# A graph network on one Trainium2 core: the two count banks of a step evicted at its end and stored by one transfer of four blocks

## The reference

```python
def L0(x, edge, src, dst, W_e, b_e, eps, W1, b1, gamma, beta, W2, b2):
    m = relu(edge @ W_e + b_e + x[src])                # one row of 128 for each edge
    h = segment_sum(m, dst, n) + (1.0 + eps) * x
    z = h @ W1 + b1
    z = relu((z - mean(z, 0)) * rsqrt(var(z, 0) + 1e-5) * gamma + beta)
    return z @ W2 + b2

def L1(x, src, dst, W0, b0, W1, b1, W2, b2):           # self loops are added to the edges
    deg = segment_sum(ones, dst, n); norm = rsqrt(deg)[src] * rsqrt(deg)[dst]
    for W, b in ((W0, b0), (W1, b1), (W2, b2)):
        x = relu(segment_sum((x @ W)[src] * norm, dst, n) + b)
    return x

x = layernorm(x + L0(x, edge_attr, src, dst, ...))
x = layernorm(x + L1(x, src, dst, ...))
```

## Time and profile before

| | |
|---|---|
| median of 3 runs | 3333.89 us (3331.76 to 3340.97) |
| the profiled execution | 3360.1 us, its span 3358.2 us |
| PE busy | 2531.0 us, 75% |
| DVE busy | 2436.1 us, 73% |
| PE weight loads busy | 2016.8 us, 60% |
| ACT busy | 1571.9 us, 47% |
| POOL busy | 1556.9 us, 46% |
| stores of `adj` | 392, 245.0 KB each |
| loads of edge features | 196, 256.0 KB each |

### The profile page before, as it was taken

The page is one execution under the profiler, slowest core; times in us unless marked ns, Lnnn a source line. Parts: engine busy times, 40 slices in busy tenths (PEclk is TensorE's granted clock), DMA queues, the critical chain, the costliest instruction groups (busy, mean ns, idle before and its releaser), DMA issues.

```text
span 3358.2 us, 43285 instructions
## 1 busy us (share of the span) xinstructions
PE 2531.0 (75%) x13163; PEld 2016.8 (60%) x13291; DVE 2436.1 (73%) x4239; ACT 1571.9 (47%) x2892; POOL 1556.9 (46%) x1694
## 2 busy tenths in 40 slices
PE   3666676666666666676666666666789999999998
PEld 2555555555555555555555555555578888888887
DVE  7777777777777777777777777777778885445554
ACT  3444444444444444444444444444555555445444
POOL 7666666666666666666666666665110000000111
PEclk7877877878778788777877878778889999999999
DMA  5333333333333333333333333333223332333442
GB/s 200 106 109 110 109 112 109 109 109 108 108 109 111 109 112 110 109 111 110 109 109 109 108 109 111 110 112 102 85 102 140 150 132 113 150 132 126 170 171 81
DMA packets 157600, 394.53 MB, mean 117 GB/s; under 512 B 37056, under 2 KB 100571, under 8 KB 151995
## 3 DMA queue, kind: packets, MB, share of 16 engines
q1 hardware_dynamic: 104332, 274.85, 21.8%
q0 software_dynamic: 51168, 105.71, 13.7%
q10 hardware_dynamic: 1872, 11.13, 0.8%
HBM read 286.75 MB, written 104.80 MB: 117 GB/s over the span
## 4 chain that ended last, share of the span: by engine, by line
DVE 50%; PE 27%; another core or an unknown queue 15%; issue 6%; ACT 1%; DVEq 1%; DMA 0%; POOL 0%; ACTq 0%; POOLq 0%; SPq 0%
DVE z L1272 21%; PE psE L1128 13%; PE psA L1128 12%; DVE work L1254 7%; DVE held L1266 6%; DVE work L1279 6%; DVE onehot L1260 4%; DVE work L1280 4%; PE psA L1083 1%; ACT wide L917 0%; PE psA L1052 0%; DVE acc L1284 0%; PE psE L1040 0%; PE psA L1040 0%
## 5 line engine op out<-in xcount | busy, mean ns | idle before, releaser
L775 POOL DMA_INDIRECT work<-in_x_flat,idx x1568 | 1494.5, 953 | 839.6 <-issue 421.7
L439 PE MATMUL psE<-we,work 128*128 128x256 f32 x1568 | 682.6, 584 | 216.8 <-DMA work<-in_edge_cols 147.7
L843 ACT ACTIVATE z<-psA 128x490 int32 x392 | 223.7, 571 | 1243.7 <-PE psA L1005 931.1
L1272 DVE TENSOR_SCALAR z<-iota_r,key,scale 128x490 bf16<-128x490 f16 x1568 | 716.0, 520 | 0.0
L439 PEld LDWEIGHTS psE<-we,work 128*128 128x128 f32 x1568 | 481.7, 307 | 146.6 <-issue 53.4
L1005 PE MATMUL psA<-z 128*128 128x245 bf16 x3136 | 459.1, 292 | 68.5 <-issue 64.7
L849 ACT ACTIVATE z<-iota_c,low 128x128 bf16<-128x128 f16 x1568 | 476.9, 389 | 0.0
L1284 DVE TENSOR_TENSOR acc<-psS,acc 128x144 f32 x196 | 60.3, 308 | 545.1 <-remote 543.7
L1128 PE MATMUL psE<-wide,halves 128*128 128x500 f32 (+1 forms) x2058 | 448.6, 375 | 5.8 <-ACT halves L932 5.4
L989 PE MATMUL psS<-onehot,work 128*128 128x72 f32 x3136 | 391.5, 279 | 80.9 <-DVE acc L1284 66.9
L436 PE MATMUL psE<-edge_bias,ones_b 128*128 128x512 bf16 x264 | 153.4, 581 | 395.2 <-DMA work<-in_edge_cols 304.8
(11 more groups left out here) (174 smaller groups left out, 2233.8 us busy)
## 6 DMA issues: line engine op xcount, KB each, us to landing
counts<-adjacency SPq DMA_DIRECT2D x36, 3062.5 KB, 9.9
adjacency<-work SPq DMA_DIRECT2D x392, 245.0 KB
work<-in_edge_cols SPq DMA_DIRECT2D x196, 256.0 KB
work<-in_x_flat,idx POOLq DMA_INDIRECT x1568
counts<-adjacency SPq DMA_DIRECT2D x3, 1592.5 KB, 6.6
acc<-in_x_cols ACTq DMA_DIRECT2D x1, 3136.0 KB
xn<-in_x_rows ACTq DMA_DIRECT2D x1, 3136.0 KB
x_spill<-xn SPq DMA_DIRECT2D x12, 256.0 KB, 2.2
```

The costliest lines, as they stand in the source:

```text
L439: mm = pe.matmul(psE0[0:n, 2 * q:2 * q + 2, :].rearrange("p j f -> p (j f)"), eaT[:, slot, q, 0:n], we[:, :], start=False, stop=True, skip ...
L775: gp.indirect_dma_start(gath[0:size(g), g % R, j, :], None, x_flat[:, :], bass.IndirectOffsetOnAxis(ap=idx[0:size(g), g, j:j + 1], axis=0) ...
L843: act.activation(taken[:, w % TAKEN, :, :], ring[:, bass.ds(at, 2 * HC)].rearrange("p (a n) -> p a n", a=ODD), ACT.Copy).then_inc(evac_ok, 1)
L1272: ve.tensor_scalar(hot[:, k % RB, :], iota_r[:, :, 0:2 * HC // ODD], key[:, k:k + 1], scale[:, k:k + 1], ALU.is_equal, ALU.mult).then_inc( ...
```

## The change

The unit of eviction and storing becomes the step. PE counts `chunk_mm` once a step, with the last matmul of the fourth pair, and waits for the evictions of the whole step before, ahead of its third pair (there the first bank is cleared that the step before may still hold). ACT makes the low one-hots first and evicts both banks behind each other at the step's end. DVE takes both apart as before, one in the middle of a step and one after the window's add; `full` has four slots. SP stores two banks, four blocks, with one transfer of 3920 bytes a partition, one register and one wait for the store before; the ring of semaphores has two. The tables hold for each step the two banks behind the block that the next step starts in, and one place for the store, so `adj` has 323 blocks a row instead of 321, and the first real block is number 4. DVE clears two banks at the start instead of one. `full` moves down in `work`, into space that the edge features' slots leave free.

```diff
--- before.py
+++ after.py
@@ -29,10 +29,9 @@
 LB = 4
 RE = 2
 RING = 5
-BEHIND = 2
 ENDS = "DAPDADAPDADAP"
 TAKEN = 4
-SLOTS = 3
+SLOTS = 4
 ODD = 5
 FLAG_STEP = 20
 PC = 7
@@ -82,14 +81,14 @@
     NB = cdiv(N, 512)
     NB4 = cdiv(NT, 4)
     NB8 = cdiv(NT, 8)
-    assert G == GF + 1 and REST % P == P // 2 and NBLK * D <= NP and 2 * HP == J and NT % PC == 0 and 2 * HC <= FREE_COL and F == P
+    assert G == GF + 1 and NBLK % 2 == 1 and REST % P == P // 2 and NBLK * D <= NP and 2 * HP == J and NT % PC == 0 and 2 * HC <= FREE_COL and F == P
     assert len(ENDS) == NB4 and FE == P // 2 and H == 2 * P and 0 < G1 < P and CH - NCHK == XB and GF * J < NCHK <= CH and J == 8 and RB % J == 0
 
     hws = nc.dram_tensor("hws_scratch", (NP, F), F32)
     x1s = nc.dram_tensor("x1_spill", (NP, F), F32)
     degs = nc.dram_tensor("degree_scratch", (NT, P), F32)
     tscr = nc.dram_tensor("table_scratch", (2 * P, 4 * HP), I32)
-    adj = nc.dram_tensor("adjacency", (P, NBLK + 8, HB), U8)
+    adj = nc.dram_tensor("adjacency", (P, NBLK + 10, HB), U8)
 
     with ExitStack() as ctx:
         def sb(name, shape, dt=F32):
@@ -186,7 +185,7 @@
 
         hot = zf[:, 0:RB * HC].bitcast(BF16).rearrange("p (r n) -> p r n", r=RB)
         lows = zf[:, RB * HC:RB * HC + LB * J * P // 2].bitcast(BF16).rearrange("p (s q n) -> p s q n", s=LB, q=J)
-        full_at = 4096 + RE * J * P
+        full_at = 4096 + RE * HP * P
         full = work[:, full_at:full_at + SLOTS * 2 * HC].bitcast(U16).rearrange("p (s b h n) -> p s b h n", s=SLOTS, b=2, h=2)
         taken_at = RB * HC + LB * J * P // 2
         taken_row = 2 * HC // ODD
@@ -263,7 +262,7 @@
         chunk_mm = sem("chunk_mm")
         evac_ok = sem("evac_ok")
         apart_ok = sem("apart_ok")
-        stored = [sem(f"stored{i}") for i in range(SLOTS)]
+        stored = [sem(f"stored{i}") for i in range(2)]
         mlp_mm = sem("mlp_mm")
         z_ok = sem("z_ok")
         bn_ok = sem("bn_ok")
@@ -696,22 +695,22 @@
                              tscr[0:G, 3 * HP + i * HQ:3 * HP + (1 + i) * HQ].rearrange("g (r i) -> r g i", r=1)).then_inc(tab_in, 16)
             sp.wait_ge(tab_in, 48)
 
-            def store(w, at):
-                sp.wait_ge(apart_ok, w + 1)
-                if w >= 1:
-                    sp.wait_ge(stored[(w - 1) % SLOTS], 16 * ((w - 1) // SLOTS + 1))
-                sp.dma_start(adj[:, bass.ds(at, 2), :].rearrange("p a n -> p (a n)"),
-                             full[:, w % SLOTS, :, :, :].rearrange("p b h n -> p (b h n)").bitcast(U8)).then_inc(stored[w % SLOTS], 16)
+            def store_four(s):
+                at = number(SPE, tab[2:3, HQ * s:HQ * s + 1], 0, NBLK + 6)
+                if s == G - 1:
+                    sp.sem_inc(tab_read, 1)
+                sp.wait_ge(apart_ok, HQ * s + HQ)
+                if s >= 1:
+                    sp.wait_ge(stored[(s - 1) % 2], 16 * ((s - 1) // 2 + 1))
+                h = HQ * (s % 2)
+                sp.dma_start(adj[:, bass.ds(at, 4), :].rearrange("p a n -> p (a n)"),
+                             full[:, h:h + HQ, :, :, :].rearrange("p s b h n -> p (s b h n)").bitcast(U8)).then_inc(stored[s % 2], 16)
 
             for s in range(G + 1):
                 if s + RE < G:
                     load_ea(sp, s + RE)
                 if s >= 1:
-                    at = numbers(SPE, tab[2:3, HQ * (s - 1):HQ * s], 0, NBLK + 6)
-                    if s == G:
-                        sp.sem_inc(tab_read, 1)
-                    for i in range(HQ):
-                        store(HQ * (s - 1) + i, at[i])
+                    store_four(s - 1)
 
             either(sp, SPE, 0, general_sum_sp)
 
@@ -719,8 +718,8 @@
             sp.wait_ge(deg_out, 16)
             sp.dma_start(degt[:, :], degs[:, :]).then_inc(deg_in, 16)
 
-            for i in range(SLOTS):
-                sp.wait_ge(stored[i], 16 * ((HQ * G + SLOTS - 1 - i) // SLOTS))
+            for i in range(2):
+                sp.wait_ge(stored[i], 16 * ((G + 1 - i) // 2))
             for lay in range(3):
                 for b in range(NCB):
                     q = unit(lay, b, 0)
@@ -737,7 +736,7 @@
                         sp.wait_ge(wide_ve, shares_ve(q - PIECES - 1))
                         sp.wait_ge(wide_act, q - PIECES)
                     nb = blocks_in(b)
-                    sp.dma_start(counts[b_slot(q)][:, 0:nb, :], adj[:, CB * b + 2:CB * b + 2 + nb, :]).then_inc(a_in[b_slot(q)], 16)
+                    sp.dma_start(counts[b_slot(q)][:, 0:nb, :], adj[:, CB * b + 4:CB * b + 4 + nb, :]).then_inc(a_in[b_slot(q)], 16)
                     if lay == 2 and b >= 3:
                         store_rows(sp, b - 3)
             for b in range(NCB - 3, NCB):
@@ -837,14 +836,14 @@
             rectify(0)
 
             def evacuate(w, at):
-                act.wait_ge(chunk_mm, w + 1)
+                act.wait_ge(chunk_mm, w // HQ + 1)
                 if w >= TAKEN:
                     act.wait_ge(apart_ok, w - TAKEN + 1)
                 act.activation(taken[:, w % TAKEN, :, :], ring[:, bass.ds(at, 2 * HC)].rearrange("p (a n) -> p a n", a=ODD), ACT.Copy).then_inc(evac_ok, 1)
 
             def low_hots(s):
                 if s >= LB:
-                    act.wait_ge(chunk_mm, HQ * (s - LB + 1))
+                    act.wait_ge(chunk_mm, s - LB + 1)
                 for q in range(J):
                     ins = act.activation(lows[:, s % LB, q, :], iota_c[:, 0:P], ACT.Abs, bias=low2[:, J * s + q:J * s + q + 1], scale=-1.0)
                 ins.then_inc(off_ok, 1)
@@ -859,10 +858,10 @@
                 at = numbers(ACTE, tab[1:2, HQ * s:HQ * s + HQ], 0, (RING - 1) * 512)
                 if s + 1 < G:
                     rectify(s + 1)
-                evacuate(HQ * s, at[0])
                 if s + 2 < G:
                     low_hots(s + 2)
-                evacuate(HQ * s + 1, at[1])
+                for i in range(HQ):
+                    evacuate(HQ * s + i, at[i])
 
             either(act, ACTE, 0, general_sum_act)
 
@@ -994,9 +993,8 @@
                 if p % HP == 0:
                     pe.wait_ge(low_ok, p // HP + 1)
                 pe.wait_ge(chunk_ok, 2 * p + 2)
-                w = p // 2
-                if p % 2 == 0 and w > BEHIND:
-                    pe.wait_ge(evac_ok, w - BEHIND)
+                if p % HP == 2 and p > HP:
+                    pe.wait_ge(evac_ok, HQ * (p // HP))
                 if p % 2 == 0:
                     pe.matmul(ring[:, FREE_COL:][:, bass.ds(clear_at, 1)], lows[:, (p // HP) % LB, 2 * p % J, :], ones_b[:, 0:1],
                               start=True, stop=True)
@@ -1004,7 +1002,7 @@
                     for half, at in enumerate((even_at, odd_at)):
                         mm = pe.matmul(ring[:, HC * half:][:, bass.ds(at, HC)], lows[:, (k // J) % LB, k % J, :], hot[:, k % RB, HC * half:HC * half + HC],
                                        start=(k < 1 and half < 1), stop=True, skip_group_check=(k >= 1 or half >= 1))
-                if p % 2 == 1:
+                if p % HP == HP - 1:
                     mm.then_inc(chunk_mm, 1)
 
             pe.wait_ge(base_ok, 2)
@@ -1150,7 +1148,7 @@
             link(ve.tensor_scalar(ident[:, :], iota_c[:, 0:P], pid[:, 0:1], None, ALU.is_equal))
             ve.tensor_scalar(diagonal[:, :], iota_c[:, 0:DIAG], pid[:, 0:1], float(DIAG_AT), ALU.subtract, ALU.is_equal
                              ).then_inc(ident_ok, 1)
-            link(ve.memset(psA[:, RING - 1, :], 0.0))
+            link(ve.memset(psA[:, RING - 2:RING, :], 0.0))
             ve.wait_ge(be_in, 16)
             link(ve.tensor_copy(be_parts[:, 0, :], be[:, 0, :]))
             link(ve.tensor_tensor(be[:, 1, :], be[:, 0, :], be_parts[:, 0, :], ALU.subtract))
@@ -1186,19 +1184,20 @@
             link(ve.tensor_scalar(second[:, :, :], second[:, :, :], MAGIC, None, ALU.add))
             link(ve.tensor_scalar(second[:, :, :], second[:, :, :], -MAGIC, None, ALU.add))
             upper = second[:, :, 1:HP + 1]
-            next_four = second[:, :, :].rearrange("p t (q two) -> p t q two", two=2)[:, :, 1:HQ + 1, 1]
+            after = second[:, :, HP + 1:HP + 2]
             link(ve.scalar_tensor_tensor(odd[:, :, :], upper, -2.0, here_, ALU.mult, ALU.add))
             link(ve.tensor_tensor(bank[:, :, 0:HP], upper, odd[:, :, :], ALU.add))
             link(ve.tensor_copy(bank[:, :, HP:2 * HP], upper))
             link(ve.scalar_tensor_tensor(bank[:, :, 2 * HP:3 * HP], upper, 1.0, odd[:, :, :], ALU.add, ALU.add))
-            link(ve.tensor_scalar(bank[:, :, 3 * HP:3 * HP + HQ], next_four, RING - 1.0, None, ALU.add))
+            for i in range(HQ):
+                link(ve.tensor_scalar(bank[:, :, 3 * HP + i:3 * HP + i + 1], after, float(RING - HQ + i), None, ALU.add))
             link(ve.tensor_scalar(round_of[:, :, :], bank[:, :, :], 1.0 / RING, 0.5 / RING - 0.5, ALU.mult, ALU.add))
             link(ve.tensor_scalar(round_of[:, :, :], round_of[:, :, :], MAGIC, None, ALU.add))
```

(6 more changed lines are left out.)

## The result

The kernel after takes 3343.2 us (median of 17 runs, 3340.0 to 3346.8), the kernel before 3336.2 us (17 runs, 3331.8 to 3341.0): a ratio of 1.002, 95% interval 1.0014 to 1.0027. That is 7.1 us more, where 1.4 us were forecast. It is inside the forecast's own range of 3328 to 3344, near its upper end, and inside the 0.3% that counts as no change, but the interval of the ratio excludes 1. So the question is where some 6 us beyond the forecast come from.

A forecast was written before the change was run, and what follows sets the result against it. The prediction took PE's late release, held back by eight gathers a step, as the bound. Terms of 0 for the steps, +0.17 at the start and +1.23 at the end gave 3335.3 us on the median 3333.9; range 3300 to 3350, no-change 3328 to 3344.

The forecast's parts named there:

- What bounds the kernel: Stage of 196 steps: PE's updates reaching three engines late set the 11.85 us step, not DVE's 9.0 us of work.
- The loop of release: In each step: release, a batch of eight gathers, about 2 us until PE's updates get through, release.
- the `find_bad` step: Step with 13 more small DVE instructions: DVE's wait shrank from 2.88 to 0.35 us, yet the step took 11.92 us.
- Evictions moved: Both ACT evictions at the step's end: cost 0, bounds 0; margins 0.3 us for the take-apart, 0.5 us for PE.
- One store of four blocks: SP's doubled store ahead of the edge load: load up to 0.67 us later; cost 0, bounds 0 and 0.67 a step.
- +0.17 at the start: Kernel start: one small linked instruction more on DVE's chain for the tables, 0.17 us.
- At the end 1.23 us: Kernel end: both evictions wait and DVE has two take-apart pairs behind the first, not one; 1.23 us, bounds 0.6 and 3.
- The edge load as bound: Slower rival: PE's chain from the edge load holds the release, 0.67 us in 193 steps, +129, 3464 us; chance 0.12.
- PE's backlog: Faster rival: PE's pending updates set the release; one update and wait less save 0 to 69 us, 3300 us; chance 0.20.
- The small slower form: Slower rival: late eviction uses up the 0.3 us margin, costs 0.1 us in most steps, up to 3350; chance 0.10.

The follow-up runs named there:

- half_gathers: Kernel before with four row gathers a step instead of eight from the fifth step on: 2792.7 us, ratio 0.832, where the kernel before took 3357.1 us.
- two_stores_again: Kernel after with two stores of two blocks at the step's end, where the kernel before took 3357.1 us: 3357.6 us, ratio 1.0001.
- the second comparison: Both kernels run again unchanged on one chip: before 3333.1 us, after 3343.8 us, ratio 1.0025.
- two_stores: Kernel after with two stores of two blocks instead of one of four, where the kernel before took 3019.6 us: 3007.5 us, ratio 0.996.
- merged_only: Kernel before with one store of four blocks a step, evictions left in place, where the kernel before took 3019.6 us: 3004.9 us, ratio 0.9952.
- all three gaining kernels: After with two stores (0.996), before with one store of four blocks (0.9952), after with flag-clearing matmuls issued twice (0.9945).
- a near copy of it: Kernel after with each one-column flag-clearing matmul issued twice, where the kernel before took 3018.9 us: 3002.5 us, ratio 0.9945.
- after_again: Kernel after, unchanged, run again for its trace beside the kernel before: 3343.8 us, ratio 1.0025.
- before_again: Kernel before, unchanged, run again for its trace: 3333.1 us.

## Why the prediction was right, and where it wasn't

The number was right with 0.8 us to spare in the forecast's own range. That the steps as a whole stood still was in part luck: long steps weren't foreseen, and that short ones pay back most of them wasn't worked out.

*What bounds the kernel.* Right for late chips. The loop of release, eight gathers and some 2 us more stands in every late trace: POOL's waits of 1.9 to 2.3 us, DVE's of 2.6 to 2.9. "That the gathers hold the updates back is inferred" is now shown by half_gathers: four gathers less a step take 564 us away, 2.96 us in each of some 190 steps, down to DVE's 8.87. That DVE has 2.9 us to spare on a late chip still rests on the `find_bad` step alone, since the run with more DVE work met a prompt one. What the text didn't see is that this holds on some chips only. On prompt ones the loop is open, POOL's gathers are the bound, and DVE is only 1.2 us behind.

*Evictions moved.* Cost 0, bounds 0: right on the second late chip, by two_stores_again; on the first, where the rhythm is, the evictions weren't tried without the large store. The pair stands 0.6 to 4 us behind the add in 155 of after's 196 steps; in the other 41, most of them next to a long step, it is later.

*One store of four blocks.* Here the sum failed. I priced one thing, the bytes ahead of the edge load, at up to 0.67 us a step. The slip is there, 0.3 us, and it costs nothing in such a step: in usual steps of the second comparison the edge product starts 3.7 us behind the load's issue instead of 3.4 and 5.85 us behind the add instead of 5.54 (medians), while the usual step went from 11.69 to 11.65. In two_stores_again it starts 6.6 us behind the add, and the step is 11.83. What I left out was that the steps aren't alike. The step's length was read from an execution in which they happened to be; the rule "the step doesn't move, so the stage doesn't" has no place for a release that slips through within a batch and then is paid for with sixteen gathers in a row and a step of 19 us. That such steps come once in twelve in both kernels, and through the whole stage only with the change, is measured. What brings them is not settled. The large store is one reading (two stores on a late chip have none). But after and two_stores were measured on two different late chips: on the first even the kernel before has the rhythm for a time, and on the second it may be absent whatever the kernel. Evictions, counts and store changed together where the rhythm was seen, so each of them is left as its cause.

*Start and end.* +0.17 at the start can't be seen (first add 65.9 against 66.1 us). At the end 1.23 us: from the last add to the end of the last take-apart it is 1.1 us more between the two late executions (5.21 and 6.35), 1.4 without gathers. The real cost of the end was another, the 5 us of step 191, the last one with gathers behind it: a long step costs little where short ones can follow, and all of its excess where none can.

*The rivals.* The edge load as bound (+129 us) and PE's backlog (-35 us) both fell. The small slower form, up to 3350, had the right size, but not its mechanism: the late evictions it spoke of are a consequence of the long steps, and half or more of the cost lies in one step. The Trainium skill's rule (Perfetto Trace Analysis, section DMA Optimizations) that larger transfers carry less overhead doesn't show as queue time: on prompt chips SP's queue took 24.9% of the engines' time with 104332 packets and 25.0% with 76108, and a packet of 1960 bytes took 85 ns on the mean, one of 3920 bytes 181 (two_stores and merged_only, 200 to 1700 us). The 0.5% gained there may come from the stores standing together and not in the middle of the step, which all three gaining kernels share; no trace of the kernel before was taken on a prompt chip, so this is only argued.

## What to carry to other kernels

When an engine waits for a count that its giver finished long ago, look at what else is in flight up to the moment it arrives, and take half of it away: one run told a cause worth 564 us from its rival. One profiled execution shows one pattern of steps; before a "0 per step" is multiplied by 196, look at a second execution, and ask what a single irregular step costs at the end of the stage. And ask whether the chip of the trace is like the others: this change is +0.2% on one late chip, and a near copy of it -0.5% on a prompt one.

## What the runs showed of the hardware

The same kernel takes 3016 to 3020 us on three chips and 3334 to 3357 us on two. The difference lies in the stage with gathers alone: with four gathers a step on a late chip it is 2792.7 us, without any on prompt chips 2791.2 and 2793.2. On late chips, in the kernel before, TensorE's counts for the window, the edge product and the first chunks arrive together, 0.1 us from one to the next, some 0.4 to 0.6 us behind the last landing of a batch of gathers. DVE's counts aren't held up: in after_again ACT's `rectify` starts 0.03 us behind the end of DVE's sum (median of 152 waits), gathers or not. In the long step shown TensorE itself stalls behind "issue" while the gathers run, 0.4 to 1.9 us ahead of a matmul. The traces of late chips also hold fewer records of counts (12402 in before_again, 42512 in two_stores on a prompt chip), so a landing there is known from a few of its sixteen increments. What in the chip does all this, and why on some only, no run here shows.
